# Ternary sets redistributed over the block products of a one-core graph and FFN kernel, with the weight blocks and x1 rows loaded at other places of the SP queue

## What is computed

```
xn = layernorm(x)                                   # x: 1250 x 1024
h  = relu(xn @ Ws0 + mean_neighbours(xn) @ Wn0 + b0)   # 20000 edges
g  = h @ Ws1 + mean_neighbours(h) @ Wn1 + b1
m  = linear attention over 16 heads of xn (relu q, relu k), then @ Wo + bo
x1 = x + g + m
n  = layernorm(x1)
y  = x1 + bitlinear(gelu(bitlinear(n, w1)), w2)     # w1: 4096 x 1024, w2: 1024 x 4096
bitlinear(a, w): a rounded row by row to integers in -128..127,
                 w rounded to -1, 0, +1 times mean(|w|)
```

## Time and profile before

| | |
|---|---|
| Median of 3 runs | 1322.86 us (1322.69 to 1328.53) |
| Profiled execution | 1321.59 us, its span 1319.8 us |
| PE busy | 1296.3 us, 98% |
| DVE, ACT, POOL busy | 833.5, 661.5, 90.7 us |
| DMA | 269.10 MB, mean 204 GB/s |
| Chain that ended last | PE 82%, DMA 6%, DVE 5%, SP queue 3% |

### The profile page before, as it was taken

The page is one execution under the profiler, slowest core; times in us unless marked ns, Lnnn a source line. Parts: engine busy times, 40 slices in busy tenths (PEclk is TensorE's granted clock), DMA queues, the critical chain, the costliest instruction groups (busy, mean ns, idle before and its releaser), DMA issues.

```text
span 1319.8 us, 18778 instructions
## 1 busy us (share of the span) xinstructions
PE 1296.3 (98%) x6370; PEld 615.3 (47%) x6370; DVE 833.5 (63%) x1467; ACT 661.5 (50%) x905; POOL 90.7 (7%) x91
## 2 busy tenths in 40 slices
PE   9999999999999999999999998998999999999999
PEld 5454445555445444444444443443444444344444
DVE  6854541352677778966983662543546988786774
ACT  7765665355213246523433663854742377464460
POOL 0000000000000002200000111431220100000000
PEclk9999999999999999999999999999999999999999
DMA  8498886864044566616875999998539838723523
GB/s 350 146 280 279 270 289 200 300 216 176 24 167 149 179 209 209 205 49 234 276 252 182 252 262 286 301 283 293 165 115 341 249 96 267 161 61 91 128 53 107
DMA packets 203093, 269.10 MB, mean 204 GB/s; under 512 B 110464, under 2 KB 144000, under 8 KB 199424
## 3 DMA queue, kind: packets, MB, share of 16 engines
q1 hardware_dynamic: 190432, 255.93, 61.2%
q0 software_dynamic: 1440, 5.24, 2.2%
q10 hardware_dynamic: 11136, 6.82, 2.0%
HBM read 184.33 MB, written 57.67 MB: 183 GB/s over the span
## 4 chain that ended last, share of the span: by engine, by line
PE 82%; DMA 6%; DVE 5%; SPq 3%; ACT 2%; issue 1%; ACTq 0%; POOL 0%; DVEq 0%
PE ps L2214 36%; PE ps L2495 12%; PE ps L2345 8%; PE ps L2638 8%; PE ps L2601 7%; PE ps L2536 6%; PE ps L2414 2%; DMA Zb<-blocks_scratch 2%; SPq L650 1%; PE ps L2353 1%; DMA STREAM<-in_w1t 1%; PE ps L2266 1%; DMA HL<-in_w2t 1%; DMA w1q_scratch<-STREAM 1%; PE ps L2248 1%
## 5 line engine op out<-in xcount | busy, mean ns | idle before, releaser
L2214 PE MATMUL ps<-S,XH 128*128 128x512 f16 x1440 | 317.1, 379 | 0.9 <-DVE Zb L1654 0.9
L2214 PEld LDWEIGHTS ps<-S,XH 128*128 128x128 f16 x1440 | 139.9, 98 | 165.9 <-DVE Zb L1654 3.3
L2214 PE MATMUL ps<-S,Zb 128*128 128x512 f16 x480 | 106.4, 379 | 0.0
L2345 PE MATMUL ps<-XH,S 128*128 128x512 f16 (+1 forms) x576 | 102.6, 339 | 0.0
L2214 PE MATMUL ps<-Zb,XH 128*128 128x512 f16 x432 | 94.8, 379 | 0.0
L995 ACT ACTIVATE AT<-ps 128x320 f16<-128x320 f32 x40 | 17.4, 434 | 143.4 <-PE ps L2214 143.3
L1607 DVE TENSOR_SCALAR STREAM<-tables,keys 128x320 f16 x240 | 71.2, 297 | 24.7 <-PE ps L2414 13.2
L2495 PE MATMUL ps<-XH,AT 128*128 128x512 f16 x400 | 86.7, 379 | 0.0
L2495 PE MATMUL ps<-Zb,AT 128*128 128x512 f16 x400 | 86.5, 379 | 0.0
L2345 PEld LDWEIGHTS ps<-XH,S 128*128 128x128 f16 x576 | 56.1, 98 | 47.0 <-issue 2.3
L2214 PEld LDWEIGHTS ps<-S,Zb 128*128 128x128 f16 x480 | 47.0, 98 | 54.4 <-issue 0.6
(11 more groups left out here) (315 smaller groups left out, 1988.8 us busy)
## 6 DMA issues: line engine op xcount, KB each, us to landing
STREAM<-in_w_all SPq DMA_DIRECT2D x48, 512.0 KB, 5.1
STREAM<-in_w1t SPq DMA_DIRECT2D x46, 512.0 KB, 5.2
STREAM<-in_w2t SPq DMA_DIRECT2D x28, 512.0 KB, 5.3
XIN<-in_x SPq DMA_DIRECT2D x20, 512.0 KB, 5.1
Zb<-in_w1t SPq DMA_DIRECT2D x14, 512.0 KB, 7.6
blocks_scratch<-S SPq DMA_DIRECT2D x4, 1792.0 KB, 8.5
blocks_scratch<-STREAM SPq DMA_DIRECT2D x4, 1792.0 KB, 8.6
S<-blocks_scratch SPq DMA_DIRECT2D x7, 1024.0 KB, 10.1
```

The lines of the kernel that those rows point to most:

```text
L2214: last = mm(acc[:, n * BANK:(n + 1) * BANK], left(l, kc), right(kc, r)[:, n * BANK:(n + 1) * BANK], start=(kc == 0 and i == 0), stop=(kc = ...
L2345: last = mm(ps[:, 3 * j * BANK + a:3 * j * BANK + b], Wq_s[:, kc, l, mc], XH[:, r, kc, a:b], start=(kc == 0 and l == 0 and r == 0), stop=( ...
```

## The change

It spreads the sets anew. Item 0 gets none, item 1 set 11, item 2 sets 12 to 14, item 3 sets 15 to 17, item 4 none, item 5 18 and 19, item 6 20 and 21, item 7 22 and 23, item 8 24 to 26, item 9 27 and 28. Sets 29, 30 and 31 are worked on in the x1 stage: by ACT behind tiles 0, 1 and 3, by DVE one tile later, stored by SP three tiles later; the load of set 31 stands just ahead of the store of set 29. For these three DVE does only its first operation and POOL takes the other one over. Set 12 now uses the buffer SPLIT, 13 HL, 14 STREAM, and so on.

On SP the loads of sets 12 and 13 come ahead of the B11 block; B21 comes ahead of the store of set 17, the other five blocks behind it, then the load of set 20. The x1 rows of tiles 0 and 1 for the second FFN product are loaded behind `x1_moves(8)` and `x1_moves(9)` and no longer behind the transpose of tile 9; the 1 MB block B22 of w2 is loaded behind that transpose instead of in the x1 stage. On DVE the addition of tile 9 moves into the scaling of tile 8, behind its maximum.

```diff
-LAST_QUADS = 30
+LAST_QUADS = 29
...
-            return 2 if i <= EDGE_QUADS else 2 + (i - EDGE_QUADS - 1) % 3
+            return 2 if i <= EDGE_QUADS else 2 + (i - EDGE_QUADS) % 3
...
-        ST_COUNTS = (1, 2, 3, 3, 1, 1, 2, 2, 2, 2)
+        ST_COUNTS = (0, 1, 3, 3, 0, 2, 2, 2, 3, 2)
...
-        X1_QUADS = {1: 30, 3: 31}
+        X1_QUADS = {0: 29, 1: 30, 3: 31}
...
+                if i == EDGE_QUADS + 1:
+                    sp.wait_ge(S("h_turned1"), 64 * PAIRS)
                 if i == EDGE_QUADS + 2:
-                    sp.wait_ge(S("h_turned1"), 64 * PAIRS)
-                if i == EDGE_QUADS + 3:
                     sp.wait_ge(S("h_turned0"), 32 * PAIRS)
...
-            block_load(sp, 1, "B11")
             quad_load(EDGE_QUADS + 1)
             quad_load(EDGE_QUADS + 2)
-            quad_load(EDGE_QUADS + 3)
-            quad_store(EDGE_QUADS)
-            def st_quads(i):
-                for n in ST_QUADS[i]:
-                    if n + 3 < LAST_QUADS:
-                        quad_load(n + 3)
-                    quad_store(n)
-            for i in range(1, PAIRS - 1):
-                st_quads(i)
-            for name, product in zip(LOAD_ORDER[1:], ("P1", "P2", "P6", "P7", "P5", "P3")):
-                sp.wait_ge(S("st_ps"), st_done(PAIRS - 1, product))
-                block_load(sp, 1, name)
-            for i in range(PAIRS - 1, 2 * PAIRS):
-                st_quads(i)
+            block_load(sp, 1, "B11")
+            def st_quad(n):
+                if n + 3 < LAST_QUADS:
+                    quad_load(n + 3)
+                quad_store(n)
+            def z1_block(n):
+                sp.wait_ge(S("st_ps"), st_done(PAIRS - 1, ("P1", "P2", "P6", "P7", "P5", "P3")[n]))
+                block_load(sp, 1, LOAD_ORDER[1 + n])
+            last_s1 = ST_QUADS[PAIRS][0] - 1
+            for n in range(EDGE_QUADS, last_s1):
+                st_quad(n)
+            z1_block(0)
+            quad_store(last_s1)
+            for n in range(1, 6):
+                z1_block(n)
+            quad_load(last_s1 + 3)
+            for n in range(last_s1 + 1, LAST_QUADS):
+                st_quad(n)
...
-            for n in range(LAST_QUADS, N_QUADS):
-                quad_load(n)
+            for n in range(2):
+                quad_load(LAST_QUADS + n)
             for b in range(2):
-                sp.wait_ge(S(f"made_out{b}"), 16 * LAST_QUADS // 2)
+                sp.wait_ge(S(f"made_out{b}"), 16 * ((LAST_QUADS + 1 - b) // 2))
...
                 x2T_turn(t, t % 2)
-                if t - 1 in X1_QUADS:
-                    quad_store(X1_QUADS[t - 1])
-                if t == 6:
-                    for b in range(2):
-                        sp.wait_ge(S(f"made_out{b}"), 16 * N_QUADS // 2)
-                    sp.dma_start(w2_in_S0, w2q_d[:, 12 * D:16 * D]).then_inc(S("B22_in"), 16)
+                if t - 3 in X1_QUADS:
+                    i = X1_QUADS[t - 3]
+                    if i + 2 < N_QUADS:
+                        quad_load(i + 2)
+                    quad_store(i)
...
             x1_moves(8)
+            sp.wait_ge(S("out0"), 16 * 4)
+            x1_load(0)
...
             x2T_turn(8, 0)
+            for b in range(2):
+                sp.wait_ge(S(f"made_out{b}"), 16 * N_QUADS // 2)
...
             x1_moves(9)
+            sp.wait_ge(S("out1"), 16 * 4)
+            x1_load(1)
...
             x2T_turn(9, 1)
+            sp.dma_start(w2_in_S0, w2q_d[:, 12 * D:16 * D]).then_inc(S("B22_in"), 16)
...
-            for t in range(2):
-                x1_load(t)
...
-            for i in range(ST_QUADS[PAIRS][0], N_QUADS):
+            def all_blocks(i):
+                made = blocks_made(i)
+                pool.wait_ge(S("made"), 2 * i + 1)
+                nc.gpsimd.tensor_tensor(made[:, 4:8:2, :], made[:, 1:4:2, :], made[:, 0:2, :], ALU.subtract,
+                                        saturate=False).then_inc(S("made"), 1)
                 last_blocks(i)
+            for i in range(ST_QUADS[PAIRS][0], LAST_QUADS):
+                last_blocks(i)
+            for i in range(LAST_QUADS, N_QUADS):
+                all_blocks(i)
...
-                cuts = {0: (0, 0, 0, 0, 2, 4), 1: (0, 0, 0, 0, 4, 8)}.get(i, (2, 4, 5, 6, 10, 12))
+                cuts = {1: (2, 2, 2, 2, 4, 4)}.get(i, (2, 4, 5, 6, 10, 12))
...
-            def quad(i):
+            def quad(i, both=True):
...
+                if not both:
+                    return
...
-            def x2_scaled(t):
+            def x2_scaled(t, after_max=lambda: None):
...
                 link(V.tensor_reduce(col("y_max"), x2n, AXX, ALU.max, apply_absolute_value=True))
+                after_max()
...
-                    quad(X1_QUADS[t - 1])
+                    quad(X1_QUADS[t - 1], both=False)
...
-            x2_scaled(8)
-            x1_rows(9)
+            x2_scaled(8, lambda: x1_add(9))
+            x1_stats(9)
```

More of the change, by code:

```diff
@@ L675, in w2_load, with x1_load @@
                              w2q_d[:, 4 * D * part:4 * D * (part + 1)]).then_inc(S(f"{name}_in"), 16)
+            def x1_load(t):
+                sp.dma_start(x1_in[:, t % 2, :], rows(x1_d, t)).then_inc(S(f"rows_in{t % 2}"), 16)
             for j in range(2):
@@ L692, in _ @@
             x2T_turn(9, 1)
+            sp.dma_start(w2_in_S0, w2q_d[:, 12 * D:16 * D]).then_inc(S("B22_in"), 16)
             for j in range(2):
                 sp.wait_ge(S(f"out{j}"), 8 * NT)
-            def x1_load(t):
-                sp.dma_start(x1_in[:, t % 2, :], rows(x1_d, t)).then_inc(S(f"rows_in{t % 2}"), 16)
-            for t in range(2):
-                x1_load(t)
             for p in range(NT // 2):
@@ L1700, in quad @@
                 wait(dve, f"made_out{i % 2}", 16 * (i // 2))
+                if i > LAST_QUADS:
+                    dve.wait_ge(S("made"), 2 * i)
                 dve.wait_ge(S("rounded"), 4 * i + 4)
@@ L1915, in st_dve @@
                     z1_lo_rest(i - 1)
-                quad(quads[0])
+                for n in quads[:1]:
+                    quad(n)
                 if i >= PAIRS:
@@ L1940, in _, with x1_add @@
             z1_lo_rest(2 * PAIRS - 1)
-            def x1_rows(t):
+            def x1_add(t):
                 j = t % 2
@@ L1950, in x1_rows, with x1_stats @@
                                        ALU.mult, ALU.add).then_inc(S("x1"), 1)
+            def x1_stats(t):
+                j = t % 2
                 dve.wait_ge(S("x1"), t + 1)
@@ L1956, in x1_rows @@
                 V.bn_aggr(mv[:, :], st[:, :]).then_inc(S("ln_mv"), 1)
-            def x2_scaled(t):
+            def x1_rows(t):
+                x1_add(t)
+                x1_stats(t)
+            def x2_scaled(t, after_max=lambda: None):
                 dve.wait_ge(S("ln_std"), NT + t + 1)
```

## The result

| | before | after |
|---|---|---|
| Median, same chip, 14 executions each | 1322.78 us (1320.28 to 1328.53) | 1331.63 us (1327.26 to 1337.23, and one of 4890 us that is left out) |
| Ratio, 95% interval | | 1.0061 [1.0045, 1.0077] |
| Profiled execution, its span | 1321.6, 1319.8 us | 1337.2, 1335.4 us |

A forecast was written before the change was run, and what follows sets the result against it. TensorE was taken as the bound, busy 1296.3 of 1319.8 us, leaving some 23 us between matmuls. 1321.6 − 16.2 + 16.8 − 2.6 + 0 = 1319.6 for the execution, 1320.9 us for the median, range 1311 to 1330.

The forecast's parts named there:

- part 1: Block products: sets spread anew over the items, removing waits in items 0 and 1 and slow clock, 8.6 us.
- half clock: TensorE at 1.2 instead of 2.4 GHz behind a long wait; 1.6 us lost each time.
- C: Length from the FFN's first P6 to the end; forecast 1.0 us shorter than before.
- part 4: Second FFN product: x1 rows loaded earlier, so two PE waits go; 2.6 us less, bounds 3.5 and 0.
- the FFN stall: Before the first FFN product: the copy waits for set 31's store behind tile 6's transpose; P6 15.2 us late.
- A: Length of the block products, first product to first edge sum; forecast 183 us, 199.5 before.
- Part 2: Block products, item 5: six second-weight blocks sent between the stores on SP arrive in time; 6.6 us go.
- Part 3: Sets 29 to 31 in the x1 stage: late store delays the first FFN product, 16.8 us more with slow clock.
- Rival (a): First FFN copy hardly waits, set 31's load and store being early enough: 1314.0, or 1304.1 without stall; chance 0.20 together.
- Rival (b): Block products: DMA engines, not SP's order, set block arrival; items 2 to 5 still wait: 1332.1 us, chance 0.15.
- Rival (c): Item 3: store of set 16 is held, first block goes late, item 5 keeps its 7 us: 1328, chance 0.12.

The follow-up runs named there:

- the changed kernel's second profile: The changed kernel profiled and timed again without an edit: median 1333.6 us, ratio 1.0097 to the kernel before.
- the wait on POOL: Changed kernel with POOL's first accumulating DMA of the block products held until pair 4's transposes landed: 1325.5 us, ratio 1.0023 to the kernel before.
- the second part alone: Kernel before, with only the first weight block moved ahead of item 3's last set store and the other five directly behind it: 1317.3 us, ratio 0.9955.
- the third part undone: Changed kernel with only sets 30 and 31 in the x1 stage, stored one tile later, their sums on DVE: 1315.9 us, ratio 0.994.
- a wait on ACT: ACT's four 1 MB block loads held behind pair 3's transposes: 1334.9 us in the changed kernel, 1326.6 in the kernel before; also used in later combined kernels.

## Why the forecast was wrong, step by step

**The step that failed is in part 1**: "The three sets of items 2 and 3 are what items 2 and 3 had before, with no wait of PE over 0.3 us, so I add nothing". The number of sets was the same, but what ACT's slack had to cover was not. Two things had changed ahead of it. Set 12 had moved to a buffer that comes free with pair 4's transposes, and POOL's accumulating DMA had lost the set that held it back and ran beside those transposes. The load came at 820.46 instead of 809.27, and item 2 paid 5.81 us, 6.0 from start to start, and 2.7 of half clock (two products, 5.30 and 2.94 instead of 2.75), 8.7 together. Forecast 1319.6 for an execution, and 8.7 added, make 1328.3; the profiled execution of this shape took 1331.0. Of the 2.7 that are left, 0.7 are at the first P6 (1.25 against 0.58). C was forecast 1.0 shorter than before (1.6 of half clock against 2.6) and was 1.2 longer in that execution, which is 2.2: 1.4 are what part 4 did not give, and 1.1 are half clock behind the FFN stall, which cost 2.7 us there and not 1.6. The first four groups of four matmuls took 6.17 us from start to start, in the kernel before 3.46 (1055.17 to 1058.63). The lines of the changed kernel's second profile, then of the kernel before:

```profile
1063.42 1.89 PE L2633 MATMUL ps<-S,tables 128*128 128x512 fp8e4 x4 [11.90 <-ACT Zb L1227]
...
1069.59 1.03 PE L2633 MATMUL ps<-S,keys 128*128 128x512 fp8e4 x4
```

```profile
1058.63 1.03 PE L2601 MATMUL ps<-S,keys 128*128 128x512 fp8e4 x4
```

That makes the sum too large by 0.5. The sum is of one execution; the medians are 10.7 and 12.7 above the forecast 1320.9, and of this the wait on POOL took away 6.1 to 8.1. The text had named the condition ("if a load comes later than that slack"), but laid no time for it, and it went past what POOL was released from. That is what taking a set away does: it also takes away the delays it gave to what stood behind it.

**Part 1's gain itself came**: the waits at 802, 808 and 827 are in no profile of the changed kernel. With the new waits taken off too, A is 187.3 us at best; forecast 183.3. What is left in that profile is mainly the wait at the first P6 (1.85 against 0.58) and one for a block in item 5 (2.19).

**Part 2** was forecast at 6.6; alone it gave 5.6 in the median and 7.2 in the stretch of the profile that it works on. In the changed kernel item 5 kept one wait for a block in some profiles (1.96 at 902.80), and none in others.

**Part 3** was right in mechanism and size: 15.3 us for the start of P6 against 15.2, and 16.3 to 18.3 and 17.7 us in the runs that send its transfers early or leave the part out, against 16.8. Half clock behind it cost 1.4 us in the first profile (three groups in 4.02 us instead of 2.59) and 2.7 in the second. Rival (a), that the copy hardly waits, falls.

**Part 4** was forecast at 2.6. Its two waits fell from 2.6 to 1.3 us (1.4 in the second profile), and in the kernels without the FFN stall C is 0.8 to 1.5 shorter than before: with the rows there, DVE waits next for tile 9's transpose, which its sums need:

```profile
1145.19 1.23 DVE L2104 TENSOR_TENSOR HL<-HL,AT 128x2048 f16<-128x2048 f16 x1 [2.13 <-DMA S<-HL]
```

The question "what is late next" was not asked here. x1_add(9) is the zero it was costed at: 0.3 and 1.3 us of PE's waits in line 2633 with the third part undone, where 0.9 and 0.5 stood before.

**Rival (b)** gave 1332.1, the number that was measured, but by another sum. It kept the waits of items 4 and 5 and decided by a block that comes over 18.1 us late; the run with the second part alone refutes that. What is true in it is that transfers were in each other's way and that a load in item 2 came late; what suffered first was a transpose in item 0. Rival (c) is half true. SP sent the first block directly behind the store of set 16, as (c) has it:

```profile
876.94 0.53 SPq L503 DMA_DIRECT2D w2q_scratch<-STREAM  x1
877.51 0.66 SPq L355 DMA_DIRECT2D S<-blocks_scratch  x1
```

Its slot was free when P1 of item 4 ended, at about 869.6, so it went 7.9 us late (6.4 in the second profile; 14.0 in the kernel before, 877.66 against 863.7). It was asked for at 892.91 and was there. The delay is real, but the 7 us that (c) leaves in item 5 were not: item 5 waited 1.96 us for another block, or not at all.

**The 12.5 us of the first profile** look like a meeting of two queues. They make up most of the 16.8 us by which A lies above the forecast 183.3 there: 11.9 more at P6 than before, 2.9 of half clock behind it (products of 5.30 and 3.14 us), 2.1 for the block in item 5. In eight profiles without a wait on ACT there, the time from SP's issue of pair 3's transposes to ACT's issue of the block loads goes with P6's wait, the shorter the longer, but for the order of the first three: 4.2, 4.1 and 3.7 us go with 0.83, 0.92 and 0.58; 3.1 with 1.25; 2.9 with 1.93; 2.8 with 3.83; 2.1 (twice) with 12.5. With ACT's blocks behind the transposes, in five profiles, P6 waited 2.34 to 4.64 and never 12. The program up to there is the same in both kernels. Whether the kernel before falls into this in some executions, too, no profile shows; its slowest of 70 took 1330.2 us. Why the transposes are sent up to 2 us earlier or later stays open.

## To carry to other kernels

When a change takes work away from a place, list what stood behind that work on each queue and is now released earlier, and ask what it will run beside; a wait on a semaphore can be worth more than the earlier start. When a buffer rotation shifts by one, look up for each of the first users what frees its new buffer. And a store that a later stage waits for belongs where its data is ready, not behind the next synchronous step of the same queue.

## What the runs showed of the hardware

DMA transposes of one queue landed late beside bulk traffic from others: 4.0 us from issue to landing without POOL's two accumulating DMAs of 512 KB, 10.1 (median) beside them, and 15.8 for the second transpose of a pair when four 1 MB loads were issued from another queue 2.1 us behind the first. With 3.1 us between them the pair took 4.1. The Trainium skill (Advanced Engine Details and Errata, X-Bar Transpose) calls transposing DMAs as fast as ordinary ones; no run here compares the two kinds alone, but beside traffic 4.0 became 10.1.

DVE's scaling took 2.52 us instead of 0.81 while POOL did its 128x1024 fp8 operation (2.01 us), where a POOL operation of half the size (1.10 us) had made it 1.61; the timelines of DVE and of POOL:

```profile
1024.14 2.52 DVE L1993 TENSOR_SCALAR HL<-TMP,mv,cols 128x1024 f32<-128x1024 f32 x1
```

```profile
1024.11 2.01 POOL L792 TENSOR_TENSOR Zb<-Zb 128x1024 fp8e4<-128x1024 fp8e4 x1 [4.54 <-DVE Zb L1722]
```

Three such meetings cost DVE 3 x 1.7 = 5.1 us, where the prediction had at most 2.4 (twice 0.8, and 0.8 more). In the kernel before the scaling met POOL as well, so only 0.9 us of it are new, against 1.25 that DVE gave away: from the start of the set's first operation on DVE to the end of the scaling it is 3.85 us (1022.81 to 1026.66), before 4.20 (1021.71 to 1025.91). The move is thus worth 0.35 us a set to DVE and not 1.2. The Trainium skill (GPSIMD Engine Reference, 8. Key points) has the two share their SBUF interfaces; the trace agrees, and the loss grew with POOL's operation in these two sizes.
